# One layer on one core: the feed-forward part three steps later, its weights spread over the fill, and the scores of all heads in one go

## The reference

```python
xx = concat([x[:, 1:2], x[:, :-1]], 1) - x
r, k, v = ((x + xx * mix_i) @ W_i.T for each of r, k, v)
g = sigmoid((x + xx * mix_g) @ W_g.T)
state = state * w + k[..., :, None] * v[..., None, :]   # per head, 16 heads of 16, over time
attn  = einsum('bhij,bhj->bhi', state, r)
x1 = layernorm(x + layernorm(attn * g @ W_o.T) * gamma + beta)
h  = silu(fp4(x1) @ fp4(w_gate).T) * (fp4(x1) @ fp4(w_up).T)    # 704 wide
out = layernorm(x1 + fp4(h) @ fp4(w_down).T)
```

## Time and profile before

| | |
|---|---|
| median of three runs | 659.39 us |
| the profiled execution, its own time | 656.57 us |
| its span, first to last instruction | 654.6 us |
| PE busy | 569.1 us (87%) |
| DVE busy | 510.9 us (78%) |
| ACT busy | 277.2 us (42%) |
| POOL busy | 330.4 us (50%) |
| granted TensorE clock, mean | 0.959 of full |

### The profile page before, as it was taken

The page is one execution under the profiler, slowest core; times in us unless marked ns, Lnnn a source line. Parts: engine busy times, 40 slices in busy tenths (PEclk is TensorE's granted clock), DMA queues, the critical chain, the costliest instruction groups (busy, mean ns, idle before and its releaser), DMA issues.

```text
span 654.6 us, 14594 instructions
## 1 busy us (share of the span) xinstructions
PE 569.1 (87%) x5120; PEld 477.9 (73%) x5120; DVE 510.9 (78%) x1506; ACT 277.2 (42%) x637; POOL 330.4 (50%) x471
## 2 busy tenths in 40 slices
PE   1468589999999999999999999999999999987754
PEld 1356467888878888888888888888888888876643
DVE  2988667888878888888888888888788888778751
ACT  1235255444444455444445444444445544432211
POOL 2234344555555555555555555555565555544321
PEclk9687689999999999999999999999999999999896
DMA  7300000000000000000000000000000000000000
GB/s 191 102 2 1 9 10 3 1 18 17 19 17 18 18 17 19 18 17 18 17 11 9 17 18 19 18 17 17 18 18 18 9 11 10 9 10 10 9 9 20
DMA packets 14046, 13.13 MB, mean 20 GB/s; under 512 B 2576, under 2 KB 13712, under 8 KB 13968
## 3 DMA queue, kind: packets, MB, share of 16 engines
q1 hardware_dynamic: 13968, 12.13, 6.2%
HBM read 7.93 MB, written 4.19 MB: 19 GB/s over the span
## 4 chain that ended last, share of the span: by engine, by line
PE 79%; DVE 9%; ACT 5%; POOL 2%; issue 2%; DMA 1%; SPq 0%; DVEq 0%; POOLq 0%; ACTq 0%
PE bank L734 20%; PE bank L867 14%; PE bank L677 9%; PE bank L752 9%; PE bank L716 4%; PE bank L804 4%; PE bank L759 4%; PE bank L769 4%; PE bank L859 3%; ACT hq_t L591 3%; PE bank L704 2%; DVE mix L1044 2%; PE bank L694 1%; POOL rstd L353 1%; PE bank L814 1%
## 5 line engine op out<-in xcount | busy, mean ns | idle before, releaser
L371 POOL TENSOR_SCALAR_AFFINE_SELECT scores<-scores 128x512 f32<-128x512 f32 x128 | 89.0, 708 | 81.0 <-ACT scores L508 80.4
L867 PE MATMUL bank<-down_t,hq_t 128*128 128x256 f32 x384 | 94.1, 396 | 21.6 <-ACT hq_t L591 21.6
L353 POOL TENSOR_TENSOR rstd<-veps,neg_half 128x1 f32<-128x1 f32 x96 | 77.8, 810 | 66.9 <-DVE veps L994 66.1
L867 PEld LDWEIGHTS bank<-down_t,hq_t 128*128 128x128 f32 x384 | 72.0, 194 | 38.3 <-ACT hq_t L591 29.4
L1044 DVE SCALAR_TENSOR_TENSOR mix<-shift,mu,x_t 128x128 f32<-128x128 f32 x256 | 82.5, 374 | 2.6 <-POOL shift L380 2.6
L508 ACT COPY scores<-bank 128x512 f32<-128x512 f32 x128 | 68.8, 590 | 34.5 <-PE bank L677 32.7
L752 PE MATMUL bank<-mix,proj_t 128*128 128x128 f32 x512 | 70.2, 295 | 10.5 <-DVE mix L1044 10.5
L734 PE MATMUL bank<-gu_hi,xq_hi 128*128 128x352 f32 x256 | 68.4, 349 | 11.2 <-DVE late L1092 6.4
L380 POOL TENSOR_TENSOR shift<-x_t 128x256 f32<-128x256 f32 x32 | 20.1, 629 | 112.6 <-ACT x_t L529 111.3
L752 PEld LDWEIGHTS bank<-mix,proj_t 128*128 128x128 f32 x512 | 66.1, 209 | 12.1 <-DVE mix L1044 11.1
L677 PE MATMUL bank<-r_par,rv 32*128 32x256 f32 x512 | 72.5, 400 | 0.8 <-ACT scores L508 0.8
(11 more groups left out here) (123 smaller groups left out, 1160.2 us busy)
## 6 DMA issues: line engine op xcount, KB each, us to landing
x_tok<-in_L_attn_x_dram SPq DMA_DIRECT2D x32, 128.0 KB, 2.3
out_dram<-late_down SPq DMA_DIRECT2D x32, 128.0 KB, 1.7
late_down<-in_L_ffn_w_down_dram SPq DMA_DIRECT2D x1, 704.0 KB, 8.6
late<-in_L_ffn_w_gate_dram SPq DMA_DIRECT2D x1, 640.0 KB, 7.1
late<-in_L_ffn_w_up_dram SPq DMA_DIRECT2D x1, 640.0 KB, 7.3
scores<-in_L_attn_W_r_dram SPq DMA_DIRECT2D x1, 256.0 KB, 5.0
scores<-in_L_attn_W_v_dram SPq DMA_DIRECT2D x1, 256.0 KB, 5.3
scores<-in_L_attn_W_g_dram SPq DMA_DIRECT2D x1, 256.0 KB, 5.5
```

Of the source, the lines that this page charges most:

```text
L353: g.tensor_tensor(rstd[:, i:i + 1], veps[:, i:i + 1], neg_half, ALU.pow).then_inc((rstd_ready, x_rstd, y_rstd)[i], 1)
L371: g.affine_select(out=a, in_=a, compare_op=ALU.is_ge, fill=0.0, base=0, pattern=[[0, 4], [1, P]], channel_multiplier=-1).then_inc(s_masked, 1)
L867: mm = t_.matmul(B_PA[:, 0:C], hq_t[:, t.c % 2, j], down_t[:, j], start=(j == 0), stop=(j == NH - 1))
```

## The change

`FFN = 3`: everything of the feed-forward part, and the last norm and the store, is done three steps later (lags 8, 9 and 10 instead of 5, 6 and 7), so there are 42 steps. x1 and xq get eight buffers for it. `xgrid` is done for tile c - 5, a step later, and its seven instructions are written each ahead of the same one of `hgrid`. `scores_of` does all 16 heads at once in four PSUM banks (`B_PA`, `B_PB`, `B_S0`, `B_S1`, four groups of 32 rows of the array), after `outs_of`; before it did two halves of eight heads in two banks. Since `B_PA` and `B_PB` hold the projections of tile c - 1, the scores now wait for their readers, `kd` among them. The transposes of the hidden activation (`h_tr`) come between the two halves of `gate_up`, no longer after both. Of the weight pieces, 0 and 1 are rounded after step 0, piece n in step n - 1 between other work; they are turned after steps 3, 6 and 7, and the low parts of gate and up are made from an SBUF copy (`gu_full`), no longer from PSUM. Tile 0 is transposed ahead of the tables. The order of the mixes, of the norms and of GpSimd's and ScalarE's work changes as the diff shows.

```diff
-LAG_MAX = 7
+FFN = 3
+LAG_MAX = 7 + FFN
...
+def turn_at(stage, general):
+
+    return 0 if general else (3, 6, 7)[stage]
...
+        s_bank = (B_PA, B_PB, B_S0, B_S1)
...
+        gu_full = sb("gu_full", [P, KC, HID])
...
-                t = tile(7)
+                t = tile(7 + ffn)
                 if t is not None:
                     rstd_of(t, 2, general)
...
-                t = None if general else tile(2)
-                if t is not None:
-                    mask(t, 0)
-                t = tile(4)
-                if t is not None:
-                    rstd_of(t, 1, general)
-                t = None if general else tile(2)
-                if t is not None:
-                    mask(t, 1)
-                t = tile(6)
+                t = tile(6 + ffn)
                 if t is not None:
                     wait(pool, hquant_step, t.count(QN, QN))
                     wait(pool, h_tr, t.count(1, -1))
                     nb = HID // BLK
                     g.tensor_tensor(blocks(hq[:, t.c % 2, 0:HID], nb), blocks(h_grid, nb),
                                     per_block(h_scale, nb), ALU.mult).then_inc(hq_ready, 1)
+                if not general:
+                    scale_x(tile(5), general)
...
                 t = None if general else tile(2)
                 if t is not None:
+                    mask(t, 0)
+                    mask(t, 1)
                     mask(t, 2)
                     mask(t, 3)
...
             def move_gate_up(m):
 
                 n = 5 + 4 * m
+                wait(act, gu_lo_ready, KC * m)
                 for k in range(KC):
                     for lo, hi in ((0, 512), (512, HID)):
                         act.wait_ge(w_tr, n + 1)
-                        s.copy(gu_hi[:, k, m * HID + lo:m * HID + hi], w_bank[n % 2][:, 0:hi - lo]
-                               ).then_inc(gu_hi_ready, 1)
-                        act.wait_ge(w_moved, n + 1)
+                        cols = slice(m * HID + lo, m * HID + hi)
+                        s.copy(gu_hi[:, k, cols], w_bank[n % 2][:, 0:hi - lo]).then_inc(gu_hi_ready, 1)
+                        s.copy(gu_full[:, k, lo:hi], w_bank[n % 2][:, 0:hi - lo]
+                               ).then_inc(w_moved, 1)
                         n += 1
...
                                  ).then_inc(sg_ready, 1)
+                t = tile(7 + ffn)
+                if t is not None:
+                    wait(act, rstd2_ready, t.count(1, 1))
+
+                    wait(act, y_stored[t.c % 2], t.affine(16 * TPB // 2, 16 * (t.c // 2) + 1))
+                    normalised(y_out[:, t.c % 2], u2, 2, y_ready)
                 t = None if general else tile(2)
                 if t is not None:
                     score(t, 0)
                     score(t, 1)
-                t = tile(7)
-                if t is not None:
-                    wait(act, rstd2_ready, t.count(1, 1))
-
...
-                t = tile(5)
+                    score(t, 2)
+                t = tile(5 + ffn)
                 if t is not None:
                     gate(t, 0)
+                t = None if general else tile(2)
+                if t is not None:
+                    score(t, 3)
                 t = tile(4)
...
-                t = tile(6)
+                    wait(act, ln2_step, t.count(LN2, 1 - x_slots * LN2))
+                    wait(act, xquant_step, t.count(QN, 4 - x_slots * QN))
+                    normalised(x1[:, t.c], u, 1, x1_ready)
+                t = tile(6 + ffn)
                 if t is not None:
...
+                t = tile(1)
+                if t is not None:
+                    wait(act, v_tr, t.count(1, 1))
+                    wait(act, u_used, t.count(1, -3))
+                    s.copy(v_tok[:, t.c % 4], B_T[:, 0:C]).then_inc(v_tok_ready, 1)
+                t = tile(5 + ffn)
+                if t is not None:
+                    gate(t, 1)
...
+            def early(c, general):
+                for stage, turn in enumerate((lambda: turn_gate_up(0), lambda: turn_gate_up(1),
+                                              turn_down)):
+                    if c == turn_at(stage, general):
+                        if c >= 4:
+                            pe.wait_ge(ln_step, LN * (c - 4) + 4)
+                        turn()
+                        pe.wait_ge(w_moved, (9, 13, 13 + NH)[stage])
+                        if stage == 2:
...
-            def scores_of(t, half):
-
-                if half == 0:
-                    wait(pe, rv_ready, t.count(1, 1))
-                    wait(pe, r_par_ready, t.count(2, 2))
-                wait(pe, s_moved, t.count(QUADS, 2 * half))
+            def scores_of(t):
+
+                wait(pe, rv_ready, t.count(1, 2))
+                wait(pe, r_par_ready, t.count(2, 4))
+                wait(pe, sg_ready, t.count(1, 2))
+                wait(pe, kd_ready, t.count(1, 2))
+                wait(pe, ln2_step, t.count(LN2, 1 - (5 + FFN) * LN2))
+                wait(pe, h_t_ready, t.count(2, -8 - 2 * FFN))
+                wait(pe, s_moved, t.count(QUADS, 0))
                 for hf in range(KC):
-                    for i in range(2):
-                        q = 2 * half + i
+                    for q in range(QUADS):
                         rows = slice(32 * q, 32 * q + 32)
-                        mm = t_.matmul((B_S0, B_S1)[i][:, hf * 256:hf * 256 + 256],
+                        mm = t_.matmul(s_bank[q][:, hf * 256:hf * 256 + 256],
                                        rv[rows, t.c % 4, 1, hf],
                                        r_par[rows, t.c % 2, hf].rearrange("p r n -> p (r n)"),
                                        start=True, stop=True, skip_group_check=True)
...
                 t = None if general else tile(3)
                 if t is not None:
                     sums_of(t)
+                    outs_of(t)
                 t = None if general else tile(2)
                 if t is not None:
-                    scores_of(t, 0)
-                t = None if general else tile(3)
-                if t is not None:
-                    outs_of(t)
-                t = tile(5)
...
-                if t is not None:
-                    gate_up(t, 1)
-                t = tile(6)
+                    scores_of(t)
+                t = tile(5 + ffn)
+                if t is not None:
+                    gate_up(t, 0, ffn)
+                t = tile(6 + ffn)
                 if t is not None:
                     wait(pe, hq_ready, t.count(1, 1))
-                    wait(pe, rv_ready, t.count(1, 6))
+                    wait(pe, rv_ready, t.count(1, 6 + ffn))
                     if not general:
-                        wait(pe, r_par_ready, t.count(2, 12))
-                    wait(pe, sg_ready, t.count(1, 6))
-                    wait(pe, kd_ready, t.count(1, 6))
+                        wait(pe, r_par_ready, t.count(2, 12 + 2 * ffn))
...
-                t = tile(6)
+                t = tile(1)
+                if t is not None:
+                    wait(pe, rv_ready, t.count(1, 1))
+                    wait(pe, x_moved, t.count(1, 2))
+                    wait(pe, xq_t_ready, t.count(1, -3 - ffn))
+                    wait(pe, v_tok_ready, t.count(1, 0))
+                    for k in range(KC):
+                        mm = t_.transpose(B_T[:, k * P:(k + 1) * P], rv[:, t.c % 4, 1, k], ident)
+                    mm.then_inc(v_tr, 1)
+                t = tile(5 + ffn)
+                if t is not None:
+                    gate_up(t, 1, ffn)
+                t = tile(6 + ffn)
...
+            def quantize(n, k):
+
+                w = pieces[n]
+                rows, cols = w.shape
+                if k == 0:
+                    wait(dve, q_ready, n - 3)
+                    if n in (0, 3):
+                        dve.wait_ge(*((gate_loaded, 16 * 2), (ffn_loaded, 16 * 3))[n // 3])
+                if k == 3:
+                    wait(dve, q_ready, n - 1)
+                grid(k, w, q_grid[0:rows, n % 2, 0:cols], cols // BLK, q_scale[:, n % 4],
+                     q_inv[:, n % 4], q_mag[:, n % 2], q_step[n % 2], lambda i: QN * (n // 2) + i)
...
+            def early(c, general):
                 if c == 0:
-                    dve.wait_ge(ffn_loaded, 16 * 3)
-                    weights(2, 3)
-                if c == 1:
-                    weights(4, 5)
-                if c == 2:
-                    low_parts(0)
-                    weights(6, 7)
-                if c == 3:
-                    low_parts(1)
+                    dve.wait_ge(tabs_moved, 5)
+                    for n in range(0, len(pieces) if general else 2, 2):
+                        for k in range(QN):
+                            quantize(n, k)
+                            quantize(n + 1, k)
+                for m in range(2):
+                    if c == (0 if general else (4, 7)[m]):
+                        low_parts(m)
...
                 def hgrid(k):
```

(19 more changed lines are left out.)

231 lines of the change are left out of this document (105 added, 126 removed).

## The result

The changed kernel takes 826.62 us (median of 4 runs, 823.30 to 828.55), the kernel before 659.70 us (4 runs beside them, 658.94 to 662.06): a ratio of 1.2517, 95% interval 1.2465 to 1.2570. The profiled execution has a span of 825.4 us for 654.6.

The account below looks back on a forecast made before the run. A loop over kd and the scores was to replace TensorE as bound, at 22.6 us a step: -33 (fill) + 111 (22 steps) + 53 (drain) = +131 on 656.6, 787.6, shown as 790 us; range 740 to 830.

Parts of the forecast that it names:

- parts 1 to 3: Steady step: scores wait for kd, closing a loop u2, kd, scores, gate_up, gated, u2, of 21.0 us for 17.54.
- the sum: Loop length at full clock: 11.0 + 1.3 + 3.5 + 2.0 + 3.2 = 21.0 us a step.
- The disputed 1.3 us: Time of the scores with four row groups at once, taken between 1.06 and 2.12; the skill's figure gives 1.1 us.
- the lower bound: Scores in four banks: 1.06 us if all four groups run side by side.
- part 4: TensorE's 4.9 us idle time lowers the clock in most steps: 1.6 us more a step, 22.6; bounds nothing and 4.
- Rival (a): Steady steps: the loop closes but the clock stays up; 21.0 us a step, 750 us; chance 0.25.
- Rival (b): Steady steps: the low clock takes nearly all TensorE work in the loop; 25 us a step, 855 us; chance 0.07.
- part 5: Fill and drain: c = 10 begins 33 us earlier (bounds 15 and 45), drain +53 us.
- The drain: End of the kernel: +37 for three added steps, +11 for five longer ones, +5 for low clock: +53 us.
- (c): Steady steps: GpSimd's root is there in time and xgrid is cheap; 19 us a step, 700 us; chance 0.08.
- (d): Steady steps: the loop doesn't close, TensorE stays the bound at 16.1 us a step; 628 us, faster; chance 0.05.

Follow-up runs that it names:

- the run with the clock kept up: Changed kernel plus 26 thrown-away TensorE products per step ahead of the scores, in TensorE's idle time: 770.1 us.
- the scores undone: Changed kernel with scores back in two halves at their old places and the transposes behind both gate_up halves; GpSimd's masks stay moved: 759.3 us.
- the last kernel: Changed kernel with both loops open, first gate_up half and v transpose ahead of scores, feed-forward two steps later, hq transposes between second half's banks: 641.5 us.
- the run with all mixes late: Changed kernel with all eight VectorE mixes moved behind gated(0): 776.6 us.
- `kd` early: Changed kernel with kd moved ahead of u on VectorE: 735.0 us, 1.1166 of the kernel before.
- both loops open: Changed kernel with kd behind hgrid(5), GpSimd's root of the first norm ahead of the last norm's, all eight mixes behind gated(0): 690.0 us.
- the scores alone on the kernel before: Kernel before with only the four-bank scores behind outs, waiting for kd, and the masks moved behind gate_pow: 711.3 us.

## Why the prediction came out as it did

**The time.** 790 was forecast, 740 to 830, slower with 0.94; 826.6 was measured, and the mechanism is the one predicted. Between the spans the forecast was -33 in the fill, +111 in 22 steps and +53 in the drain, +131 in all; measured are -15.9, +129.9 and +56.8, +170.8. The 40 us between are 17.1, 18.9 and 3.8 us.

**The loop (parts 1 to 3).** `u2` to the end of `kd` was put at 11.0 and measured 11.06, and that is in part luck: `u` begins 5.84 us behind `u2` for the 6.8 forecast, and from there to the end of `kd` are 5.22 us for 4.2, and the two errors cancel. `u` comes sooner because `norm3`'s `veps` is at 3.68 (4.2) and the time from it to `u` is 2.16 (2.57; VectorE's idle part of it is 1.38, for the 1.5 to 2 named). The way from `u` to `kd` is longer by the R mixes, 1.72 us for 0.58. What made the mixes' price wrong is an order that I had read for VectorE and not for GpSimd. In the kernel before GpSimd's multiply for `hq` came late, behind masks; with the masks moved behind it, it starts 0.06 us after the R mixes, on data that VectorE has just finished. That the two meet is shown by the rows above. The run with the R mixes late takes them off the way to `kd`, but they don't recover there, still beside the end of the multiply and what follows it on GpSimd: the mean of one mix between 200 and 500 us is 341 ns before, 485 in the changed kernel, 531 with the R mixes late and 395 with all of them late. By the Trainium skill, "SBUF — State Buffer", section "Who interferes with whom", a VectorE instruction with two inputs in SBUF contends with a GpSimd instruction that reads SBUF, for a pair of ports that one of them holds alone; the trace agrees, as the mixes end 0.16 us after the multiply. From `kd` to the scores are 0.31 us, a term that the sum lacked. The second half took 2.06 (2.0), and from its end to the next `u2` it was 3.11 (3.2). In the run with the clock kept up the scores take 1.1 us of the loop (1.3), and from the first half of `gate_up` to the second are 3.46 (3.5). Without the low clock the step is 21.0 us, as the sum said.

**The scores' size.** The disputed 1.3 us: at the full clock, sixteen products in four banks take 1.15 us. So they lie side by side, and the lower bound was near. By the Trainium skill, "TensorE: Matmul & The Clock Gate", section "Measured speedup vs the span model", which gives 3.07 times for four row groups, the estimate is 1.1 us, and the trace agrees.

**The clock (part 4) is the mis-sized term of the step.** 1.6 us a step was forecast, 2.4 measured by taking it away; in the step shown it is 0.9 us in the scores (2.03 from their start to the next product, for 1.08) and 1.6 in the first half of `gate_up` (338.13 to 341.81, 3.68 for 2.04 in the earlier trace rows). I had taken it to come in most steps and for part of the work; it comes in every step, and for nearly all of the work until the second half. Over 22 steps the 0.8 us are 18 of the 19 us that the 22 steps lack. Rival (a), the clock stays up, is refuted by the rows, and its price is confirmed: its 750 us are 767 with the fill as it was, and the run with the clock kept up took 770. Rival (b) had the mechanism of the low level right and its length too long.

**The fill (part 5) is the other.** -33 was forecast, -15.9 measured: 17 us. Step c = 7 begins at 105.8 us for 123.9, 18 ahead, where I had counted 27 for the weights; then c = 7 to 9 took 54.7 us for 52.6, where I had counted 6 us gained. A likely reason is that the weights' rounding stands among `hgrid`, on the way to `kd`, and that the loop is closed there too, so that VectorE's waits aren't free room. The runs bear on it in part: with the scores undone c = 7 begins at 99.6 us and c = 10 at 151.0, which is 9.5 of the 17 us; what the rest is stays open.

**The drain** was +53 forecast and +56.8 measured, and its parts came out near too. By the starts of `u2`, the three steps that it has more (c = 36 to 38) take 41.4 us for 37, and the five others 15 more than before, for 16.

**The rivals (c) and (d)** are out: `kd` is done 335.79 - 324.21 = 11.6 us into TensorE's step, and it was wanted at 331.2 - 324.21 = 7.0. (d) named a point that is needed and isn't enough: with `kd` in time and nothing else changed the step is 19.5 us, and 17.0 and less only with ready work ahead of the scores and the other loops opened as well. In the last kernel TensorE is the bound with 16.3 us for the 16.1 given there. Its 628 us needed -33 in the fill and a short drain as well.

**What the prediction did not see** is the second loop, `u2` to `gated(0)`. It cost the changed kernel nothing by itself (the run with all mixes late), but it is why neither `kd` early nor the scores undone came near the kernel before.

## What to carry to other kernels

When a moved instruction gains a wait, add up the row of the engine that is waited for, from its own last fixed point, and lay it beside what the waiting engine has to do meanwhile; if that is less, the step becomes a loop over both, and repairing one hand-over only shows the next one. A loop here was broken by order, first by shortening the row ahead of the late result, then by putting ready work in front of the wait; the same operations, at the end with the feed-forward part one step sooner, gave 827 and 642 us. Read more than one step before naming a wait: the rows that I first took for a kernel's step were those of three in 22. Moving a stage later buys room in the fill and pays for each step in the drain: 13.8 us for 7.3 here.

## What the runs showed of the hardware

- Work that nothing uses made the kernel 56 us faster, since it kept the granted clock at 1.00 instead of 0.50 for some six microseconds of nearly every step.
- The length of an idle time of TensorE alone doesn't tell the level behind it. 4.9 to 5.3 us were followed by 0.50 in all 22 steps of the changed kernel; waits of 1.96 to 1.99 us in one kernel (scores undone) by 0.50 in some steps and by 1.00 in others, and so were those of 1.52 us in another (`kd` early), where a wait of 1.0 to 1.2 us lies shortly ahead; 1.74 us were followed by 0.50 with both loops open, 2.18 us by 1.00 with the scores alone on the kernel before. What TensorE had done before them differs, so these are rows and no rule.
- Two mixes of 128 elements took 1.72 us beside a GpSimd multiply of 704 elements, and 0.58 without it; the multiply itself took 1.50 us for 1.38.
